# A two-layer graph network on one core: ten score blocks instead of eleven, and x loaded transposed

## The chip, the core and the metric

The kernel runs on one core of one Trainium2 chip. The metric is the device time in microseconds: 1216.45 us, the median of three runs (1216.28 to 1217.08). TensorE is PE here, VectorE DVE, ScalarE ACT, GpSimd POOL, SyncE SP (it only issues DMAs).

## The reference

There are 16 graphs of 512 rows and 384 features (D). Each graph passes a layer norm with relu and then two layers; the result is added to x. Cut to what matters:

```python
h = jnp.maximum(_layernorm(x), 0.0)          # (x - mean) / sqrt(var + 1e-5)
def layer(h, params):
    u = einsum('bid,bjd->bij', h, h) / sqrt(D)          # scores, symmetric
    a = softmax(u);  delta = a * adj
    attn = delta / (sum(delta, -1) + 1e-10)
    hl, hs, hr = h @ wl.T + b_l, h @ ws.T + b_s, h @ wr.T + b_r
    ctx = (attn * upper) @ hl + diag(attn) * hs + (attn * lower) @ hr
    o = (ctx - mean) / sqrt(var + 1e-12) * g + beta
    return relu(o)
x = x + layer(layer(h, p0), p1)
```

## The kernel before

The graphs go in eight pairs, and a pair in four steps: steps 0 and 1 are layer 0 of its two graphs (a and b), steps 2 and 3 layer 1 of the two. The order of every engine's instructions is written out by hand, one Python block for each engine, and semaphores tie them together: an engine works strictly in its own order.

Every fp32 operand is split in a rounded part (_hi) and a rest (_lo), so that a product is three fast matmuls (`products`, L274 to L276). In a step PE does, in this order:

- **Scores** (`scores`, L314): the transposed features ht of one row tile of 128 against a range of columns, in a PSUM bank u_ps for each of the four row tiles. The matrix is symmetric: tile 0 takes all four blocks of 128 columns, tile 1 three, tiles 2 and 3 two each: eleven blocks. ACT copies blocks above the diagonal to u_off.
- **Projections** P(t, n) (`project`): row tile t with weight n. n = 0 and 1 go to proj, n = 2 (self) to hs. There are twelve, in four rotating PSUM banks (rot_ps). A unit must wait until the unit four places ahead of it has been emptied by DVE (`evacuate`).
- **Mirrors** (`mirror`, L332): behind the first two projections, five transposes of u_off fill the missing blocks.
- **M** (`spread_max`, L349), in steps 2 and 3 only, after four projections: the row maxima are turned.
- **T** (`turn_h`, L340): 12 transposes turn the features of the next step's graph. In steps 1 and 2 they turn z, the result of the step before; in steps 0 and 3 they turn x_norm, the layer-normalised x of the graph that comes next in layer 0.
- **Attend** (`attend`), four tiles i: each adds three groups of products of the other tiles' masked scores et with hw, and then those of its diagonal block dg. Its first group waits for all four et_lo, each group for its hw_lo, the diagonal for dg.

Around it, ACT takes exp of the scores, rounds e and proj to et_hi and hw_hi and normalises x (`x_normalise`); DVE masks (L617), forms et_lo (`e_low`, L622), the diagonals (L634), evacuates (L650), ends attend (`finish`) and takes x's statistics (`x_statistics`, L559); POOL forms hw_lo (`proj_low`, L881), the triangles of the diagonal block, dg (`triangles`, L893), and powers for reciprocal deviations (L898, L855).

Of the kernel before, what the change touches and what calls it, by code (L numbers as in the profile page):

```python
# [10 lines left out]
P = 128  # L11


def build_digcn(nc, x, adj_t, w_t, bl, bs, br, ln_w, ln_b, ln_w0_t, ln_b0_t, out):
# [31 lines left out]
    U_FROM = [0, 1, 2, 2]  # L46
    off_at = [0, 3 * P]
# [5 lines left out]
    TWO = (2, 2, 2, 2)  # L53
# [5 lines left out]
    N_HT = (0, 3, 3, 0)  # L59
    N_SHIFT = (1, 1, 0, 0)  # L60
# [4 lines left out]
    with ctx:  # L65
# [22 lines left out]
        u_off = sb("u_off", [P, 5 * P])  # L88
        w_stage = sb("w_stage", [P, 3 * dim])
# [30 lines left out]

        m_rows = u_off[:, 0:n_rows]
        ht_f32 = x_norm[:, :, :].rearrange("p t n -> p (t n)").rearrange("p (k n) -> p k n", n=n_rows)
# [43 lines left out]
        x_norm_loaded = sem("x_norm_loaded")  # L166
        x_loaded = [sem(f"x_loaded_{g}") for g in "ab"]
# [39 lines left out]
        w_stages = [flat(e_sb, 0, 3 * dim), flat(z, 0, 3 * dim), w_stage[:, :]]  # L207
        w_stages += [w_stage[:, :]] * KB
# [5 lines left out]
        def _(sp):  # L214
# [16 lines left out]
            sp.dma_start(x_norm[:, :, :], rows(x, 1)).then_inc(x_norm_loaded, 16)  # L231
# [6 lines left out]
            for g in range(2):  # L238
                sp.dma_start(x_sb[g][:, :, :], rows(x, g)).then_inc(x_loaded[g], 16)
            sp.wait_ge(w_lo0_done, KB)  # L240
            load_w(KB)

            def pair(it, first, last):
                if first:
                    for c in range(1, KB):
                        sp.wait_ge(w_lo1_done, c)
                        load_w(KB + c)
                for g in range(2):
                    s = 2 + g
# [19 lines left out]
        def _(pe):  # L269
# [21 lines left out]
            def step(it, s, first, last):  # L291
# [685 lines left out]
```

## Time and profile before

| what | value |
|---|---|
| time of the profiled execution | 1216.47 us |
| its span | 1214.7 us |
| PE busy | 1200.9 us, 99% |
| DVE busy | 917.0 us, 75% |
| ACT busy | 515.0 us, 42% |
| POOL busy | 561.3 us, 46% |
| PE in the chain that ended last | 93% |

The span is the part of the execution that the profile covers, from the first instruction to the last. Busy time leaves out waits for semaphores, but an instruction that is blocked while it runs counts as busy. Matmuls overlap, so what one costs in a row of them is the distance from start to start and not its duration.

### The profile page before, as it was taken

The numbers are of one execution on the slowest core, as the hardware profiler recorded it, in microseconds if no ns is written. First come the engines' busy times: TensorE is split into PE (matmuls) and PEld (weight loads), VectorE is DVE, ScalarE is ACT, GpSimd is POOL, SyncE is SP. The second block draws the span as 40 slices with busy tenths as digits, with TensorE's granted clock in tenths as the row PEclk, the third lists the DMA queues.
The fourth block names the chain that finished last, engine by engine and source line by source line (L and its number), as shares of the span: only waits on it lengthen the run. The fifth ranks groups of instructions, "written<-read, shape, count | busy, mean of one in ns | idle before, by whom it ended". The sixth has DMA issues, their size and how long they took to land.

```text
span 1214.7 us, 18788 instructions
## 1 busy us (share of the span) xinstructions
PE 1200.9 (99%) x7146; PEld 1178.6 (97%) x7146; DVE 917.0 (75%) x2034; ACT 515.0 (42%) x1061; POOL 561.3 (46%) x624
## 2 busy tenths in 40 slices
PE   9999999999999999999999999999999999999997
PEld 7899999999999999999999999999999999999997
DVE  6567995679955898558985599865997659975688
ACT  4346433355333453334543444434344353434532
POOL 4465353554534545344543354442545424544346
PEclk9999999999999999999999999999999999999999
DMA  8001320012200131001310013100231002210000
GB/s 303 21 21 37 111 79 1 1 61 88 78 2 1 61 113 53 1 1 62 113 53 1 1 62 113 53 1 1 72 103 53 1 1 93 81 53 1 1 27 27
DMA packets 37002, 60.85 MB, mean 50 GB/s; under 512 B 2352, under 2 KB 27952, under 8 KB 36912
## 3 DMA queue, kind: packets, MB, share of 16 engines
q1 hardware_dynamic: 36624, 59.26, 14.8%
q8 instruction: 56, 0.92, 0.3%
q10 hardware_dynamic: 288, 0.39, 0.1%
q14 instruction: 34, 0.28, 0.1%
HBM read 47.06 MB, written 12.58 MB: 49 GB/s over the span
## 4 chain that ended last, share of the span: by engine, by line
PE 93%; DVE 4%; ACT 1%; DMA 1%; issue 1%; POOL 0%; SPq 0%; DVEq 0%
PE rot_ps L275 16%; PE rot_ps L276 16%; PE rot_ps L274 16%; PE u_ps L274 14%; PE u_ps L276 14%; PE u_ps L275 14%; PE rot_ps L340 3%; PE u_ps L332 1%; DMA x_norm<-x_dram 1%; PE rot_ps L349 1%; DVE et_lo L622 0%; DVE proj L650 0%; DVE x_stats L559 0%; DVE z L687 0%; ACT x_norm L419 0%
## 5 line engine op out<-in xcount | busy, mean ns | idle before, releaser
L881 POOL TENSOR_TENSOR hw_lo<-proj,hw_hi 128x384 fp32r<-128x384 f32 x256 | 280.8, 1112 | 323.6 <-ACT hw_hi L471 323.6
L274 PE MATMUL rot_ps<-w_hi,ht_hi 128*128 128x384 f32 x1152 | 389.6, 338 | 1.3 <-DVE proj L650 1.3
L275 PE MATMUL rot_ps<-w_lo,ht_hi 128*128 128x384 f32 x1152 | 385.7, 335 | 0.0
L276 PE MATMUL rot_ps<-w_hi,ht_lo 128*128 128x384 f32 x1152 | 385.5, 335 | 0.0
L274 PEld LDWEIGHTS rot_ps<-w_hi,ht_hi 128*128 128x128 f32 x1152 | 216.5, 188 | 1.6 <-DVE proj L650 1.6
L275 PEld LDWEIGHTS rot_ps<-w_lo,ht_hi 128*128 128x128 f32 x1152 | 216.5, 188 | 0.0
L276 PEld LDWEIGHTS rot_ps<-w_hi,ht_lo 128*128 128x128 f32 x1152 | 216.3, 188 | 0.0
L444 ACT ACTIVATE u_off<-u_ps 128x384 f32<-128x384 f32 x64 | 28.0, 438 | 363.9 <-PE u_ps L276 363.8
L650 DVE TENSOR_TENSOR proj<-rot_ps,bias 128x384 f32<-128x384 f32 x256 | 138.5, 551 | 51.7 <-PE rot_ps L276 51.7
L471 ACT ACTIVATE hw_hi<-proj 128x384 fp32r<-128x384 f32 x256 | 125.5, 518 | 86.5 <-DVE proj L650 85.9
L893 POOL TENSOR_TENSOR dg<-et_hi,tri 128x256 fp32r<-128x256 f32 x128 | 103.4, 808 | 126.7 <-PE u_ps L276 126.7
L706 DVE SCALAR_TENSOR_TENSOR hs<-hs,e_diag,u_ps 128x385 f32<-128x385 f32 x128 | 78.2, 611 | 78.1 <-PE u_ps L276 78.1
L274 PE MATMUL u_ps<-hw_hi,et_hi 128*128 128x386 f32 x384 | 133.1, 347 | 0.5 <-DVE et_lo L622 0.5
L276 PE MATMUL u_ps<-hw_hi,et_lo 128*128 128x386 f32 x384 | 129.8, 338 | 0.0
L275 PE MATMUL u_ps<-hw_lo,et_hi 128*128 128x384 f32 x384 | 129.6, 338 | 0.0
L622 DVE TENSOR_TENSOR et_lo<-e_sb,et_hi 128x512 fp32r<-128x512 f32 x128 | 127.4, 995 | 2.5 <-ACT et_hi L475 2.5
L274 PE MATMUL u_ps<-ht_hi 128*128 128x256 f32 (+2 forms) x384 | 124.6, 325 | 0.7 <-DVE ht_lo L588 0.7
L276 PE MATMUL u_ps<-ht_hi,ht_lo 128*128 128x256 f32 (+2 forms) x384 | 124.6, 324 | 0.0
L275 PE MATMUL u_ps<-ht_lo,ht_hi 128*128 128x256 f32 (+2 forms) x384 | 124.0, 323 | 0.0
L898 POOL TENSOR_TENSOR rstd<-var_eps,minus_half 128x4 f32<-128x4 f32 (+1 forms) x35 | 34.3, 980 | 187.9 <-DVE var_eps L674 187.6
L893 POOL TENSOR_TENSOR dg<-et_lo,tri 128x256 fp32r<-128x256 f32 x128 | 113.7, 888 | 0.0
L650 DVE TENSOR_TENSOR hs<-rot_ps,bias 128x384 f32<-128x384 f32 x128 | 68.9, 550 | 31.9 <-PE rot_ps L276 31.6
(89 smaller groups left out, 2047.6 us busy)
## 6 DMA issues: line engine op xcount, KB each, us to landing
out_dram<-z SPq DMA_DIRECT2D x64, 192.0 KB, 1.9
x_norm<-x_dram SPq DMA_DIRECT2D x15, 768.0 KB, 4.4
adj_a<-adj_t_dram SPq DMA_DIRECT2D x8, 1024.0 KB, 5.3
adj_b<-adj_t_dram SPq DMA_DIRECT2D x8, 1024.0 KB, 5.5
x_a<-x_dram SPq DMA_DIRECT2D x8, 768.0 KB, 4.6
x_b<-x_dram SPq DMA_DIRECT2D x8, 768.0 KB, 4.7
w_stage<-w_t_dram SPq DMA_DIRECT2D x4, 576.0 KB, 5.4
e_sb<-w_t_dram SPq DMA_DIRECT2D x1, 576.0 KB, 4.9
```

Of the source, the lines that this page charges most:

```text
L274: pe.matmul(dst, a_hi, b_hi, start=first and m == 0, stop=False)
L275: pe.matmul(dst[:, 0:b_lo.shape[1]], a_hi, b_lo, start=False, stop=False)
L276: done = pe.matmul(dst, a_lo, b_hi, start=False, stop=last and m == n - 1)
L340: done = pe.transpose(bank(it, s, "T", db)[:, t * P:(t + 1) * P], src[:, t, db * P:(db + 1) * P], ident[:, :])
L444: act.activation(u_off[:, off_at[t]:off_at[t] + width], u_ps[t][:, (t + 1) * P:n_rows], ACT.Copy).then_inc(off_copied, 1)
L471: act.activation(hw_hi[:, t, n, 0:dim], proj[:, t % 2, n, :], ACT.Copy).then_inc(hw_hi_done, 1)
L622: dve.tensor_tensor(et_lo[:, i, :], e_sb[:, i, :], et_hi[:, i, :].bitcast(F32), ALU.subtract).then_inc(et_lo_done, 1)
L650: dve.tensor_tensor(dst, bank(it, s, "P", t, n)[:, 0:dim], bias[:, layer, n, :], ALU.add).then_inc(p_freed, 1)
L706: dve.scalar_tensor_tensor(out=hs[:, i, 0:dim + 1], in0=hs[:, i, 0:dim + 1], scalar=e_diag[:, i:i + 1], in1=u_ps[i][:, 0:dim + 1], op0=ALU ...
L881: pool.tensor_tensor(hw_lo[:, t, n, :], proj[:, t % 2, n, :], hw_hi[:, t, n, 0:dim].bitcast(F32), ALU.subtract).then_inc(hw_lo_done, 1)
L893: pool.tensor_tensor(dg[:, i % 2, part, :, :], block_t.unsqueeze(1).to_broadcast([P, 2, P]), tri[:, :, :], ALU.mult).then_inc(dg_done, 1)
L898: pool.tensor_tensor(rstd[:, cols], var_eps[:, cols], minus_half[:, cols], ALU.pow).then_inc(rstd_done, 1)
```

## The change

Two things change, with what follows from each.

- Scores: row tiles 0 and 1 take three blocks each, 2 and 3 two each, ten in all; tile 3 takes blocks 0 and 3, read and written with a gap. ACT makes four copies to u_off (256, 256, 128, 128 columns) instead of two, and PE six mirror transposes in the order of tiles 1, 2, 3, 0, behind the first projection. The first exp and the first row maximum wait for the mirror of their tile, and DVE evacuates P(0, 0) first.
- x for layer 0: there is no T on x, but for the very first graph. x is loaded a second time, transposed (xt_sb). Its rows' mean and reciprocal deviation come from x in another row layout (four successive rows in a partition), are stored to DRAM and loaded again, spread to all 128 partitions (mean_b and rstd_b, in x_norm). POOL subtracts the mean (`x_centre`, 3 instructions of 128x512), DVE multiplies by the deviation with relu (`x_scale`, 3), ACT rounds (`round_x`), DVE takes the rest (`h_low`). Before, ACT normalised x in place (4) and DVE's h_low read PSUM. The statistics of both next graphs stand in step 1 instead of steps 2 and 3. ht_f32 moves from x_norm to proj, so in steps 1 and 2 `round_h` waits for all eight hw_lo.
- Attend waits for et_lo tile by tile. Three weight chunks of layer 1 are staged in x_b.

```diff
-    UNITS_0 = [("P", *p) for p in PROJ + SELF] + TURN
-    UNITS_1 = [("P", *p) for p in PROJ[:4]] + [("M",)] + [("P", *p) for p in PROJ[4:] + SELF] + TURN
-    ORDERS = [UNITS_0, UNITS_0, UNITS_1, UNITS_1]
+    UNITS_0 = [("P", *p) for p in PROJ + SELF]
+    UNITS_1 = [("P", *p) for p in PROJ[:4]] + [("M",)] + [("P", *p) for p in PROJ[4:] + SELF]
+    ORDERS = [UNITS_0, UNITS_0 + TURN, UNITS_1 + TURN, UNITS_1]
...
-    U_FROM = [0, 1, 2, 2]
-    off_at = [0, 3 * P]
+    SCORED = [slice(0, 3), slice(1, 4), slice(2, 4), slice(0, 4, 3)]
+    OFF_BLOCKS = [slice(1, 3), slice(2, 4), slice(3, 4), slice(0, 1)]
+    OFF_AT = [0, 2, 4, 5]
+    MIRROR_ORDER = (1, 2, 3, 0)
+    MIRRORED = [[(3, 5)], [(0, 0)], [(0, 1), (1, 2)], [(1, 3), (2, 4)]]
...
+        mean_b = x_norm[:, :, :].rearrange("p t n -> p (t n)")[:, 0:n_rows]
+        rstd_b = x_norm[:, :, :].rearrange("p t n -> p (t n)")[:, n_rows:2 * n_rows]
...
-        ht_f32 = x_norm[:, :, :].rearrange("p t n -> p (t n)").rearrange("p (k n) -> p k n", n=n_rows)
+        ht_f32 = proj[:, :, :, :].rearrange("p a b d -> p (a b d)").rearrange("p (k n) -> p k n", n=n_rows)
...
+            def load_stat_rows(graph):
+                sp.dma_start(x_norm[:, :, :], stat_rows(x, graph)).then_inc(x_norm_loaded, 16)
+            def load_xt(graph):
+                sp.dma_start(xt_sb[:, :, :], x_t[graph].rearrange("(k p) n -> p k n", p=P)).then_inc(xt_loaded, 16)
+            def store_x_rows(graph):
+                sp.wait_ge(x_rstd_done, graph + 1)
+                sp.dma_start(rows_dram[graph % 2].rearrange("(q p t) -> p q t", q=2, t=TILES),
+                             x_mv[:, graph % 2, :, :]).then_inc(x_rows_stored[graph % 2], 16)
+            def spread_x_rows(graph):
+                sp.wait_ge(x_rows_stored[graph % 2], 16 * ((graph + 1) // 2))
+                sp.dma_start(flat(x_norm, 0, 2 * n_rows),
+                             rows_dram[graph % 2:graph % 2 + 1, :].to_broadcast([P, 2 * n_rows])).then_inc(x_rows_spread, 16)
...
+                next_a, next_b = it * 2 + 2, it * 2 + 3
+                if not last:
+                    sp.wait_ge(xt_scaled, KB * (next_a - 1))
+                    load_stat_rows(next_a)
+                    sp.wait_ge(ht_lo_done, LEAD_T + at(it, 0, KB, THREE))
+                    load_xt(next_a)
                 if first:
-                    for c in range(1, KB):
-                        sp.wait_ge(w_lo1_done, c)
-                        load_w(KB + c)
+                    sp.wait_ge(w_lo1_done, 1)
+                    load_w(KB + 1)
+                if not last:
+                    sp.wait_ge(x_stats_done, next_a * XS + TILES)
+                    load_stat_rows(next_b)
+                    store_x_rows(next_a)
+                    store_x_rows(next_b)
+                    spread_x_rows(next_a)
...
                         if g == 0:
+                            sp.wait_ge(xt_scaled, KB * next_a)
+                            spread_x_rows(next_b)
+                        else:
                             sp.wait_ge(ht_lo_done, LEAD_T + at(it, s, KB, THREE))
-                        else:
-                            sp.wait_ge(t_ready, LEAD_T + at(it, s, KB, THREE))
-                        sp.dma_start(x_norm[:, :, :], rows(x, it * 2 + (2 + g))).then_inc(x_norm_loaded, 16)
+                            load_xt(next_b)
...
-                    left = U_FROM[t] * P
-                    products(u_ps[t][:, left:n_rows],
+                    which = SCORED[t]
+                    products(blocks(u_ps[t][:, :], which),
                              [(a_t[0][:, kb, lo:hi], a_t[1][:, kb, lo:hi],
-                               a_t[0][:, kb, left:n_rows], a_t[1][:, kb, left:n_rows])
+                               blocks(a_t[0][:, kb, :], which), blocks(a_t[1][:, kb, :], which))
...
-                    if t < TILES - 1:
-                        pe.wait_ge(off_copied, at(it, s, min(t + 1, 2), TWO))
-                    for above in range(U_FROM[t]):
-                        lo = off_at[above] + (t - above - 1) * P
-                        done = pe.transpose(u_ps[t][:, above * P:(above + 1) * P],
-                                            u_off[:, lo:lo + P], ident[:, :])
+                    pe.wait_ge(off_copied, at(it, s, (4, 2, 3, 4)[t], N_OFF))
+                    for column, source in MIRRORED[t]:
+                        done = pe.transpose(u_ps[t][:, column * P:(column + 1) * P],
+                                            u_off[:, source * P:(source + 1) * P], ident[:, :])
...
                 project(0, 0)
+                for t in MIRROR_ORDER:
+                    mirror(t)
                 project(0, 1)
-                for t in range(1, TILES):
-                    mirror(t)
...
+                def round_x(db):
+                    graph = it * 2 + (1 if s == 0 else 2)
+                    act.wait_ge(xt_scaled, KB * (graph - 1) + (db + 1))
+                    act.activation(ht_hi[:, 1 - s % 2, db, :], xt_sb[:, db, :], ACT.Copy).then_inc(ht_hi_done, 1)
...
+                def x_scale(graph, db):
+                    dve.wait_ge(xt_centred, KB * (graph - 1) + (db + 1))
+                    dve.scalar_tensor_tensor(out=xt_sb[:, db, :], in0=xt_sb[:, db, :], scalar=0.0, in1=rstd_b,
+                                             op0=ALU.max, op1=ALU.mult).then_inc(xt_scaled, 1)
...
+                if s == 1 and not last:
+                    x_stats_of(next_a, range(TILES))
+                    x_variance(next_a)
                 if layer == 0:
+                    evacuate(0, 0)
                     mask(0)
-                    evacuate(0, 0)
                     evacuate(0, 1)
                     mask(1)
                     mask(2)
@@ -724,26 +783,30 @@
                     mask(3)
                     e_low(0)
                     evacuate(1, 1)
+                    if s == 1 and not last:
+                        x_stats_of(next_b, range(0, 2))
                     e_low(1)
                     e_low(2)
                     evacuate(2, 0)
-                    if early:
-                        dve.wait_ge(x_norm_loaded, 16)
-                        x_statistics(0)
+                    if s == 1 and not last:
+                        x_stats_of(next_b, range(2, TILES))
                     e_low(3)
+                    if s == 1 and not last:
+                        x_variance(next_b)
...
+            def x_centre(graph):
+                pool.wait_ge(xt_loaded, 16 * graph)
+                pool.wait_ge(x_rows_spread, 16 * graph)
+                for db in range(KB):
+                    pool.tensor_tensor(xt_sb[:, db, :], xt_sb[:, db, :], mean_b, ALU.subtract).then_inc(xt_centred, 1)
...
                 proj_low(1)
+                if s == 0:
+                    x_centre(it * 2 + 1)
+                if s == 2 and not last:
+                    x_centre(it * 2 + 2)
```

POOL in step 0 of the second pair, before. hw_lo<-proj is proj_low, x2 for one row tile, dg is triangles, the memset sets ones.

```order
L881 TENSOR_TENSOR hw_lo<-proj,hw_hi 128x384 x2
L876 MEMSET hs 128x4x2
L881 TENSOR_TENSOR hw_lo<-proj,hw_hi 128x384 x2
L893 TENSOR_TENSOR dg<-et_hi,tri 128x256
L893 TENSOR_TENSOR dg<-et_lo,tri 128x256
L881 TENSOR_TENSOR hw_lo<-proj,hw_hi 128x384 x2
```

The same place in the changed kernel; xt_sb<-xt_sb,x_norm is x_centre.

```order
L937 TENSOR_TENSOR hw_lo<-proj,hw_hi 128x384 x2
L932 MEMSET hs 128x4x2
L937 TENSOR_TENSOR hw_lo<-proj,hw_hi 128x384 x2
L911 TENSOR_TENSOR xt_sb<-xt_sb,x_norm 128x512 x3
L949 TENSOR_TENSOR dg<-et_hi,tri 128x256
L949 TENSOR_TENSOR dg<-et_lo,tri 128x256
L937 TENSOR_TENSOR hw_lo<-proj,hw_hi 128x384 x2
```

Three instructions of 128x512 now stand behind the second tile's hw_lo and ahead of all other hw_lo and of all dg.

DVE in step 1 of the second pair, before, from the first et_lo. proj<-rot_ps is evacuate, diag_junk the diagonal.

```order
L622 TENSOR_TENSOR et_lo<-e_sb,et_hi 128x512
L650 TENSOR_TENSOR proj<-rot_ps,bias 128x384
L622 TENSOR_TENSOR et_lo<-e_sb,et_hi 128x512 x2
L650 TENSOR_TENSOR proj<-rot_ps,bias 128x384
L622 TENSOR_TENSOR et_lo<-e_sb,et_hi 128x512
L634 SCALAR_TENSOR_TENSOR diag_junk,e_diag<-e_sb,ident 128x128
L650 TENSOR_TENSOR proj<-rot_ps,bias 128x384
L634 SCALAR_TENSOR_TENSOR diag_junk,e_diag<-e_sb,ident 128x128 x3
L650 TENSOR_TENSOR proj<-rot_ps,bias 128x384 x2
```

The same place in the changed kernel; x_stats, x_mv and x_var_eps are the statistics of x.

```order
L677 TENSOR_TENSOR et_lo<-e_sb,et_hi 128x512
L705 TENSOR_TENSOR proj<-rot_ps,bias 128x384
L605 BN_STATS x_stats<-x_norm 128x6 x2
L677 TENSOR_TENSOR et_lo<-e_sb,et_hi 128x512 x2
L705 TENSOR_TENSOR proj<-rot_ps,bias 128x384
L605 BN_STATS x_stats<-x_norm 128x6 x2
L677 TENSOR_TENSOR et_lo<-e_sb,et_hi 128x512
L611 BN_AGGR x_mv<-x_stats 128x2 x4
L615 TENSOR_SCALAR x_var_eps<-x_mv 128x4
L689 SCALAR_TENSOR_TENSOR diag_junk,e_diag<-e_sb,ident 128x128
L705 TENSOR_TENSOR proj<-rot_ps,bias 128x384
```

Nine small or middle instructions of the second graph's statistics have come between evacuate(1,1) and evacuate(2,1).

SP at the end of the loads at the start, before.

```order
L239 DMA x_b<-x_dram 128x4x384
L217 DMA w_stage<-w_t_dram 128x1152 x3
L252 DMA adj_a<-adj_t_dram 128x4x512
L257 DMA x_norm<-x_dram 128x4x384
L260 DMA out_dram<-z 128x384 x4
```

And in the changed kernel; rows_dram is the DRAM buffer of means and deviations.

```order
L283 DMA x_a<-x_dram 128x4x384
L245 DMA x_b<-w_t_dram 128x1152
L260 DMA rows_dram<-x_mv 128x2x4
L265 DMA x_norm<-rows_dram 128x1024
L253 DMA x_norm<-x_dram 128x1536
L256 DMA xt_sb<-x_t_dram 128x3x512
```

The store of rows, the load that spreads them, and the statistics' load of the next graph have come behind the last of the first loads; each waits for another engine.

## Rows read from the trace of the kernel before

**Rows 1.** Windows, steps 3, 0, 1: busy us by engine (instructions), clock, DMA
```profile
573.64:611.11 37.47, 37.47 (x226) 36.92 (x226) 35.77 (x84) 15.89 (x34) 17.10 (x19) 1.00 0.29 92
611.11:648.12 37.01, 37.01 (x222) 36.55 (x222) 27.76 (x63) 13.23 (x29) 17.30 (x19) 1.00 0.14 44
648.12:685.13 37.01, 37.01 (x222) 36.55 (x222) 22.25 (x47) 15.66 (x32) 16.42 (x18) 1.00 0.00 1
```

**Rows 2.** Timeline of PE, scores, two projections, mirrors of step 3: start us, duration us
```profile
573.64 0.39 PE L274 MATMUL u_ps<-ht_hi 128*128 128x512 f32 x1
...
575.73 0.34 PE L274 MATMUL u_ps<-ht_hi 128*128 128x384 f32 x1
...
579.46 0.34 PE L274 MATMUL rot_ps<-w_hi,ht_hi 128*128 128x384 f32 x1
...
582.59 0.71 PE L332 MATMUL u_ps<-ident,u_off 128*128 128x128 f32 x5
```

**Rows 3.** Chain in order of time, transposes of x and mirrors: start us, us
```profile
582.75 0.55 PE u_ps L332 x5
...
599.41 1.31 PE rot_ps L340 x12
```

**Rows 4.** Waits of PE: total us, times, longest us
```profile
PEld rot_ps L340 <- ACT x_norm L419: 1.7, 1, 1.7
...
PEld rot_ps L274 <- DVE proj L650: 1.6, 1, 1.6
...
PE u_ps L274 <- DVE et_lo L622: 0.5, 1, 0.5
```

**Rows 5.** Timeline of POOL in step 0
```profile
625.98 1.19 POOL L881 TENSOR_TENSOR hw_lo<-proj,hw_hi 128x384 fp32r<-128x384 f32 x1 [0.23 <-ACT hw_hi L471]
627.14 1.19 POOL L893 TENSOR_TENSOR dg<-et_hi,tri 128x256 fp32r<-128x256 f32 x1
...
632.47 0.74 POOL L893 TENSOR_TENSOR dg<-et_lo,tri 128x256 fp32r<-128x256 f32 x1
633.16 1.99 POOL L881 TENSOR_TENSOR hw_lo<-proj,hw_hi 128x384 fp32r<-128x384 f32 x2
```

**Rows 6.** Timeline of DVE in step 0
```profile
626.46 1.27 DVE L622 TENSOR_TENSOR et_lo<-e_sb,et_hi 128x512 fp32r<-128x512 f32 x1 [0.16 <-ACT et_hi L475]
...
630.79 1.12 DVE L634 SCALAR_TENSOR_TENSOR diag_junk<-e_sb,ident 128x128 f32<-128x128 f32 x1
...
631.84 1.01 DVE L650 TENSOR_TENSOR proj<-rot_ps,bias 128x384 f32<-128x384 f32 x2
```

**Rows 7.** Timeline of PE: end of projections in step 0, attend in step 2
```profile
636.25 1.47 PE L340 MATMUL rot_ps<-ident,x_norm 128*128 128x128 f32 x12
...
711.97 0.42 PE L274 MATMUL u_ps<-hw_hi,et_hi 128*128 128x386 f32 x1
```

**Rows 8.** Timeline of DVE: statistics and means in step 3, evacuate(2,1) in step 1
```profile
574.31 1.01 DVE L559 BATCH_NORM_STATS2 x_stats<-x_norm 128x6 f32<-128x384 f32 x2
...
577.11 0.37 DVE L563 BATCH_NORM_AGGREGATE x_mv<-x_stats 128x2 f32<-128x6 f32 x4
...
666.55 0.55 DVE L650 TENSOR_TENSOR proj<-rot_ps,bias 128x384 f32<-128x384 f32 x1
```

**Rows 9.** Timeline of POOL in step 2
```profile
704.82 5.30 POOL L881 TENSOR_TENSOR hw_lo<-proj,hw_hi 128x384 fp32r<-128x384 f32 x4 [1.35 <-ACT hw_hi L471]
...
710.78 1.18 POOL L893 TENSOR_TENSOR dg<-et_lo,tri 128x256 fp32r<-128x256 f32 x1
```

**Rows 10.** DMA issues, first 45 us, then all: KB each, median us to landing
```profile
x_norm<-x_dram SPq DMA_DIRECT2D x1, 768.0 KB, 6.4
...
out_dram<-z SPq DMA_DIRECT2D x64, 192.0 KB, 1.9
x_norm<-x_dram SPq DMA_DIRECT2D x15, 768.0 KB, 4.4
```

**Rows 11.** Windows: 30 to 35 us of the span
```profile
30.00:35.00 5.00, 3.92 (x23) 3.60 (x21) 4.97 (x14) 0.53 (x1) 2.22 (x2) 1.00 0.00 0
```

More of the change, by code:

```diff
@@ L198, in all_pairs, with blocks, stat_rows @@
                 body(it, it == 0, it == pairs - 1)
+        def blocks(columns, which):
+            return columns.rearrange("p (b c) -> p b c", c=P)[:, which, :]
         def rows(dram, graph):
             return dram[graph].rearrange("(t p) n -> p t n", p=P)
+        def stat_rows(dram, graph):
+            return dram[graph].rearrange("(p t) n -> p t n", t=TILES)
         def flat(tile, lo, hi):
@@ L513, in step @@
                     round_e(3)
-                    if s == 0 and not first:
-                        x_normalise(it * 2 + 2, range(0, 2))
-                else:
-                    row_sum(0)
+                else:
+                    for t in range(TILES):
+                        row_sum(t)
                     round_proj(0)
-                    row_sum(1)
-                    row_sum(2)
-                    row_sum(3)
                     copy_max()
@@ L529, in step @@
                     round_e(1)
-                    if s == STEPS - 1 and not last:
-                        x_normalise(it * 2 + 3, range(0, 2))
                 if first and s == 1:
@@ L537, in step @@
                     round_e(3)
-                if s == 0 and not first:
-                    x_normalise(it * 2 + 2, range(2, TILES))
-                elif s == STEPS - 1 and not last:
-                    x_normalise(it * 2 + 3, range(2, TILES))
                 round_proj(3)
-                if first and s == 0:
-                    x_normalise(2, range(TILES))
                 if not final:
                     for db in range(KB):
-                        round_h(db)
+                        round_h(db) if s in (1, 2) else round_x(db)
                 if first and s == 0:
@@ L601, in step, with x_stats_of @@
                 g, layer = s % 2, s // 2
[L602 to L603 removed]
+                next_a, next_b = it * 2 + 2, it * 2 + 3
+                def x_stats_of(graph, tiles):
+                    if tiles[0] == 0:
+                        dve.wait_ge(x_norm_loaded, 16 * graph)
+                    for t in tiles:
+                        x_statistics(t)
+                def x_scale(graph, db):
+                    dve.wait_ge(xt_centred, KB * (graph - 1) + (db + 1))
+                    dve.scalar_tensor_tensor(out=xt_sb[:, db, :], in0=xt_sb[:, db, :], scalar=0.0, in1=rstd_b,
+                                             op0=ALU.max, op1=ALU.mult).then_inc(xt_scaled, 1)
                 def row_max(t):
[L606 to L609 removed]
+                    dve.wait_ge(u_full, at(it, s, MIRROR_ORDER.index(t) + 1, FOUR))
                     dve.tensor_scalar(e_sb[:, t, :], u_ps[t][:, :], -scale, None, ALU.mult, ALU.min,
@@ L780, in step @@
                         diagonal(t)
-                else:
-                    for t in range(TILES):
-                        evacuate(t, 2)
-                if not final:
+                if s in (1, 2):
                     for db in range(KB):
                         h_low(db)
+                if s == 0:
+                    for db in range(KB):
+                        x_scale(next_a - 1, db)
                 if final:
@@ L807, in step @@
                         centre(i - 1)
-                    if ahead is not None and i in (1, 2):
-                        if i == 1:
-                            dve.wait_ge(x_norm_loaded, (ahead - 1) * 16)
-                        x_statistics(2 * i - 2)
-                        x_statistics(2 * i - 1)
+                    if s in (0, 3) and i < 2:
+                        for db in ((0,), (1, 2))[i]:
+                            h_low(db)
+                    if s == 2 and not last and i in (1, 2):
+                        for db in ((0, 1), (2,))[i - 1]:
+                            x_scale(next_a, db)
                 dve.wait_ge(stats_done, at(it, s, TILES, FOUR))
@@ L902, in step @@
                     pool.wait_ge(den_done, at(it, s, 0, ONE))
+                if first and s == 0:
+                    x_rstd_of(1)
+                if s == 1 and not last:
+                    x_rstd_of(it * 2 + 2)
                 proj_low(0)
@@ L908, in step @@
                     proj_low(2)
-                    if first and s == 0:
-                        x_rstd_of(2)
                     triangles(1)
+                    if s == 1 and not last:
+                        x_rstd_of(it * 2 + 3)
                     proj_low(3)
@@ L946, in step @@
                 rstd_of(slice(0, TILES), 1)
-                if s >= 2 and not last:
-                    x_rstd_of(it * 2 + (s + 1))
             all_pairs(lambda it, first, last: [step(it, s, first, last) for s in range(STEPS)])
```

174 lines of the change are left out of this document (81 added, 93 removed).

## The prediction

> **What bounds the kernel now.** First the page: the span is 1214.7 us, PE is busy in 99% of it, and the chain that ended last is PE for 93%. Then windows of one step each [rows 1]: PE fills all 37.0 or 37.5 us, at a granted clock of 1.00. DVE is busy for 35.8 of 37.5 us in step 3, but for 28 and 22 in steps 0 and 1; POOL for about 17. Then the waits: PE's own are the few of rows 4, 4 us of 1215. So whatever leaves PE is gained, until another engine becomes late, and the question is how much room its feeders have. PE needs two things of them: a free one of the four rotating banks (DVE's evacuations), and for attend et_lo from DVE, hw_lo and dg from POOL. Their dates stand in the timelines, and the main part of this prediction is to compare them with PE's.
>
> **What leaves PE.** Scores: nine 512-wide products of tile 0 take 2.09 us (573.64 to 575.73) [rows 2]; nine 384-wide ones of tile 1, read in the same timeline, 1.59 (575.73 to 577.32), 0.177 each, near the 0.174 of a projection's (3.13 us from 579.46 to 582.59 for eighteen [rows 2]). Tile 0 becomes 384 wide, tile 1 stays: 0.50 us in each of 32 steps, -16.0 us. Tile 3 now reads blocks 0 and 3. No row shows an operand with a gap; between nothing and the price of 384 columns (0.5 a step, +16 us) I take nothing, since 256 columns still stream. Turning x: 12 transposes cost 1.31 us [rows 3], in steps 0 and 3 but not in the last one: 15 x 1.31, -19.65 us. Mirrors: six instead of five, at 0.55/5 [rows 3], 32 x 0.11 = +3.5 us. PE's own work: -32.1 us. The waits of the first pair's step 0, 1.6 and 1.7 us, come from statistics between evacuations and from the normalising of x, and go: -3.3. The 0.5 us for et_lo in the last step goes too, since attend now waits tile by tile [rows 4]. Together -35.9 us.
>
> **What the feeders get.** POOL: three subtractions of 128x512 in steps 0 and 2, behind proj_low(1). DVE: three x_scale in steps 0 and 2, where it waits for attend anyway, and in step 1 all statistics of two graphs; those of steps 2 and 3 go. ACT: two short copies more, no normalising. In steps 2 and 3 the row sums stand together, but copy_max still waits for M, which PE reaches after the same projections, so what follows it keeps its dates.
>
> One POOL subtraction, alone: two hw_lo (384 columns) take 1.99 us, dg (256) 0.69 from start to start (632.47 to 633.16) [rows 5]. With 1.01 for one hw_lo that is 0.98 and 0.69, 0.0022 us a column, 1.25 us for 512 and 3.75 for three.
>
> Beside DVE it is dearer. dg takes 1.19 at 627.14 and 0.74 at 632.47; hw_lo takes 1.19 at 625.98 [rows 5]. On DVE an et_lo takes 1.27 beside them, and a diagonal, with a quarter of its columns, 1.12 [rows 6]. The starts show turns: each of these begins its work when the other engine's instruction ends. They read two tiles of SBUF; two evacuations, which read PSUM, take 1.01 together [rows 6]. The Trainium skill, "SBUF — State Buffer", section "Who interferes with whom", has this as a rule: a DVE instruction with two SBUF inputs and a GpSimd instruction that reads SBUF exclude each other for their whole length. It speaks against this change, since it puts longer instructions of GpSimd among DVE's; by it the time is the forecast's, without it rival 2's. The trace agrees, by rows 5 and 6.
>
> *Step 0* (611.11 to 648.12 [rows 1]). evacuate(0,1) now comes behind the mirrors, 0.66 later; masks and e_low(2) follow about 0.5 later. From there the engines take turns. Before, two dg and one hw_lo (0.7 + 0.7 + 1.0 = 2.4) lie between e_low(2) and diagonal(1), now three subtractions (3.75); then two dg (1.4) stand where POOL had one hw_lo and a gap. 0.5 + 1.35 + about 0.9: evacuate(3,0) starts at 634.6 instead of 631.84 [rows 6] and ends at 635.1. P(2,2), which takes its bank, would start two projections (3.13) before they all end, which is 636.25 [rows 7] + 0.11 for the sixth mirror: 633.2. Stall 2.0 us. POOL's last hw_lo ended at 633.16 + 1.99 = 635.15 [rows 5]; with 3.75 and 1.0 more of turns it is 639.9. Attend now starts at 636.36 + 2.0 and wants it for its third group, six products or 1.05 later, at 639.4: 0.5 more, with the wake-up 0.6. So 2.6 us. Bounds: without turns, 635.15 + 3.5 against 637.4, 1.3; with every subtraction at the contended 1.19 for 384 columns [rows 5], 1.6 for 512, 3.6.
>
> *Step 1* (from 648.12 [rows 1]). The second graph's statistics stand ahead of evacuate(2,1): four in 1.88 (two in 1.01, overlapping) and 0.48 for means and the sum behind them (0.37 for four means) [rows 8], 2.36 in all; 0.25 for exps that start later, 0.3 of turns. evacuate(2,1) goes from 666.55 [rows 8] to 669.45 and ends at 670.0. P(1,2) needs it three projections before their end, which comes 25.14 us after the step's start as in step 0 (636.25 - 611.11): 648.12 + 25.14 - 4.7 + 0.11 = 668.7. Stall 1.35 us; bounds 0.8 (the 2.36 alone) and 2.4. The first graph's statistics fall into DVE's wait for exp and cost nothing.
>
> *Step 2* (from 685.13). POOL idles for 1.35 us behind proj_low(1), until 704.82 [rows 9]; that takes part of the 3.75. Tile 0's last dg ended at 710.78 + 1.18 = 711.96 [rows 9]; 2.4 later is 714.4, and with 0.8 for turns with four et_lo and the diagonals 715.2. PE wants it nine products (1.66) after attend's start at 711.97 [rows 7], and 0.11: 713.7. Stall 1.5 us; bounds 0.6 and 2.5.
>
> *Step 3.* ACT is freed of 2.4 us, but the 1.31 us of PE that hid dg are gone: by the same walk it is 0.25 us late; bounds 0 and 0.5.
>
> Step 0 pays in pairs 2 to 8, steps 1 and 2 in pairs 1 to 7 (the last has no next graph), step 3 in all: seven times 2.6 + 1.35 + 1.5 + 0.25 = 5.7, 39.9 us.
>
> *First pair, step 0.* POOL waits for graph 1's spread rows. x's second load lands 6.4 us after its issue [rows 10], statistics follow, and the small store queues behind loads that run until shortly before 30 us (none from 30 on [rows 11]): landed at 28.8. No row shows a 16-byte store or the spread of one row; by size, 192 KB land in 1.9 us and 768 KB in 4.4 [rows 10], 512 KB in 3.3, so the rows are there at 32.2. Behind them POOL has 3.75, four dg and four hw_lo (6.8) to do: 42.75. Attend's third group comes at 37.6: scores end 6 us after they begin at 11.7, now 0.5 less, attend starts 19.4 later (636.36 less 611.11 + 5.82), the group 1.05 after it. Stall 5.2 us; bounds 3 and 8. In later pairs the rows have over 20 us.
>
> **Sum.** 1216.5 - 35.9 + 5.2 + 39.9 = 1225.7 us. 1216.5 is the profiled execution's own time, and within 0.1 the median. Break-even lies at (35.9 - 5.2)/7 = 4.4 us of stalls a pair.
>
> **Rivals.**
> 1. *Forecast.* The turns add up as walked: 1225.7; its own range is 1214 to 1240. For it: the same walk over steps 0 and 2 of before gives their starts within 0.2 us. Against: it chains some 20 instructions to dates with about 1 us of room.
> 2. *Faster, the work is only inserted.* If DVE and POOL meet less in the new dates, the stalls are 1.3 + 0.8 + 0.6 a pair, 18.9 in all, and 3 in the first: 1216.5 - 35.9 + 21.9 = 1202.5. Its place is e_low(2) to evacuate(3,0) of step 0, its price up to 3 us a pair, and it decides as soon as a pair's stalls are under 4.4. For it: POOL is idle for over half of each step. Against: rows 5 and 6 show the turns already.
> 3. *Faster, all hidden.* The subtractions beat hw_lo's rate and the banks come free in time; 3 us stay in the first pair: 1183.6. Against: 2.2 us more on POOL's chain of step 0 reach PE.
> 4. *Much slower, the way through DRAM.* If store and spread are so slow that POOL waits for them in step 2 too, all that is queued behind x_centre waits: hw_lo, dg, then attend. Over 20 us are left; each microsecond beyond costs 7, so 3 of them give 1247. SP, which waits in order, has adjacency and outputs behind these DMAs, with tens of microseconds.
>
> **Chances.** Forecast 0.52, rival 2 0.28, rival 3 0.12, rival 4 0.08. A difference under 0.2% (2.4 us) can't be told from no change; 0.05 of the forecast's and 0.05 of rival 2's fall there. Faster 0.35, same 0.10, slower 0.55. The range 1194 to 1240 holds the first two.
>
> **What would show it.** After: six mirrors in 0.66 us, tile 0's nine products in 1.59, tile 3's as tile 2's, no transposes of x behind the start. POOL's 512-wide group at 1.3 to 1.7 us each. PE waits for DVE's proj (P(2,2) in step 0, P(1,2) in step 1), for hw_lo in step 0 and dg in step 2. Steps 0 to 3 last 37.9, 38.0, 38.6 and 36.0 us instead of 37.0, 37.0, 37.5 and 37.5. I am wrong if PE is still busy for 99%, or if it waits for a DMA past the first pair.

## The result, and the profile after

The kernel after takes 1219.88 us (median of 7 runs, 1218.83 to 1221.22) against 1216.59 before (7 runs, 1216.28 to 1217.20): ratio 1.0028, 95% interval 1.0016 to 1.0039. It is slower by 3.3 us where 9.2 were forecast. The profiled execution took 1218.83 us, the shortest of the seven; its span is 1217.1.

First the page of the profile: PE is no longer the whole of the span. Engine, busy us, share; then the chain that ended last.

```profile
PE 1178.3 (97%) x6998; PEld 1157.8 (95%) x6998; DVE 982.9 (81%) x2064; ACT 495.1 (41%) x1065; POOL 625.7 (51%) x669
...
PE 49%; DVE 27%; POOL 10%; ACT 7%; issue 5%; DMA 2%; DVEq 0%; POOLq 0%
```

Windows of steps 0 to 3 of pair 5 show where [rows 1 for before]: PE now stands still for 1.1 us in steps 0 and 1 and 0.6 in step 2.

```profile
615.74:652.65 36.91, 35.78 (x212) 35.14 (x212) 31.08 (x59) 11.67 (x27) 20.04 (x21) 1.00 0.27 86
652.65:690.58 37.93, 36.83 (x224) 36.45 (x224) 26.34 (x65) 16.14 (x34) 18.09 (x20) 1.00 0.16 53
690.58:728.58 38.00, 37.37 (x228) 36.84 (x227) 31.09 (x62) 18.95 (x39) 21.29 (x21) 1.00 0.08 29
728.58:764.78 36.20, 36.06 (x216) 35.55 (x215) 34.30 (x73) 13.98 (x32) 16.90 (x18) 1.00 0.28 90
```

The waits of PE answer to [rows 4]: total us, times, longest. They are the three that were forecast, each at its place; two places of hw_lo's nine are the first pair's.

```profile
PE rot_ps L337 <- DVE proj L705: 13.7, 14, 1.3
PE u_ps L337 <- POOL hw_lo L937: 9.1, 9, 4.9
PE u_ps L337 <- POOL dg L949: 4.3, 7, 0.6
```

The timeline of PE has them one by one: P(2,2) and attend's third group in step 0, P(1,2) in step 1, tile 0's dg in step 2 (start us, duration, in brackets the wait ahead).

```profile
638.28 0.44 PE L337 MATMUL rot_ps<-w_hi,ht_hi 128*128 128x384 f32 x1 [0.82 <-DVE proj L705]
643.06 0.41 PE L337 MATMUL u_ps<-hw_hi,et_hi 128*128 128x386 f32 x1 [0.30 <-POOL hw_lo L937]
...
673.90 0.44 PE L337 MATMUL rot_ps<-w_hi,ht_hi 128*128 128x384 f32 x1 [1.10 <-DVE proj L705]
...
719.48 0.45 PE L337 MATMUL u_ps<-hw_hi,dg 128*128 128x386 f32 x1 [0.63 <-POOL dg L949]
```

Where the time went, from the starts of the scores in each trace (us a step, pair 5; the first pair's step 0 apart). The last five columns belong to the experiments below.

| step | before | after | scores_only | centre_late | r_turns | r_all | r_tail |
|---|---|---|---|---|---|---|---|
| 0 | 37.01 | 36.91 | 36.57 | 35.24 | 35.61 | 35.25 | 35.25 |
| 1 | 37.01 | 37.93 | 36.57 | 37.93 | 37.96 | 36.55 | 36.55 |
| 2 | 37.48 | 38.00 | 37.04 | 38.36 | 37.04 | 37.05 | 37.05 |
| 3 | 37.48 | 36.20 | 37.51 | 36.53 | 36.00 | 37.38 | 37.15 |
| first | 40.31 | 44.61 | 39.91 | 36.70 | 45.95 | 36.43 | 36.04 |

In the last pair, which prepares no next graph, steps 1 and 2 take 36.55 and 37.05: these are the lengths without stalls. For step 0, 35.25 is seen in the experiments. For step 3 its parts, each without a stall, add up: scores 5.29, projections up to attend 19.88, and attend 10.58, as in step 0 (10.65 in steps that turn h). That is 35.75, and pair 6 of the kernel after does show 35.74. So a pair loses 1.66, 1.38, 0.95 and 0.45 us, 4.44 in all, and PE's own work is 4.38 less. They cancel. (PE's waits in the views are shorter than these losses: a wait counts from the end of a product of 0.34 us, and in an unbroken row the next one starts after 0.175.)

### The profile page after: what moved, and what is told of

Read it like the earlier page. It is cut to its first block, busy times and chain, and to the rows that moved or that the text cites. A ratio compares the mean times of both kernels' runs of the same rounds, so it can differ in the third digit from the quotient of the medians.

```text
span 1217.1 us, 18750 instructions
## 1 busy us (share of the span) xinstructions
PE 1178.3 (97%) x6998; PEld 1157.8 (95%) x6998; DVE 982.9 (81%) x2064; ACT 495.1 (41%) x1065; POOL 625.7 (51%) x669
## 4 chain that ended last, share of the span: by engine, by line
PE 49%; DVE 27%; POOL 10%; ACT 7%; issue 5%; DMA 2%; DVEq 0%; POOLq 0%
PE u_ps L337 11%; PE u_ps L339 11%; PE u_ps L338 11%; DVE et_lo L677 6%; PE rot_ps L337 5%; PE rot_ps L339 5%; PE rot_ps L338 5%; POOL hw_lo L937 4%; POOL xt_sb L911 3%; DVE proj L705 3%; DVE e_sb L672 3%; DVE u_ps L684 2%; POOL dg L949 2%; DVE hs L705 2%; DVE diag_junk L689 2%
## 5 line engine op out<-in xcount | busy, mean ns | idle before, releaser
L337 PE MATMUL rot_ps<-w_hi,ht_hi 128*128 128x384 f32 x1152 | 390.9, 339 | 13.7 <-DVE proj L705 13.7
L500 ACT ACTIVATE u_off<-u_ps 128x128 f32<-128x128 f32 (+1 forms) x128 | 42.5, 332 | 392.5 <-PE u_ps L339 392.3
L677 DVE TENSOR_TENSOR et_lo<-e_sb,et_hi 128x512 fp32r<-128x512 f32 x128 | 145.0, 1137 | 1.4 <-ACT et_hi L529 1.4
L949 POOL TENSOR_TENSOR dg<-et_hi,tri 128x256 fp32r<-128x256 f32 x128 | 106.4, 831 | 70.2 <-PE u_ps L339 70.2
L954 POOL TENSOR_TENSOR rstd<-var_eps,minus_half 128x4 f32<-128x4 f32 (+1 forms) x35 | 38.7, 1107 | 185.3 <-DVE var_eps L726 185.0
L337 PE MATMUL u_ps<-ht_hi 128*128 128x256 f32 (+1 forms) x384 | 118.8, 309 | 0.7 <-DVE ht_lo L635 0.7
L339 PE MATMUL u_ps<-ht_hi,ht_lo 128*128 128x256 f32 (+1 forms) x384 | 118.8, 309 | 0.0
L338 PE MATMUL u_ps<-ht_lo,ht_hi 128*128 128x256 f32 (+1 forms) x384 | 118.3, 308 | 0.0
L949 POOL TENSOR_TENSOR dg<-et_lo,tri 128x256 fp32r<-128x256 f32 x128 | 108.9, 851 | 0.0
L337 PE MATMUL u_ps<-hw_hi,dg 128*128 128x386 f32 x256 | 88.0, 344 | 4.3 <-POOL dg L949 4.3
```

The lines of the kernel that those rows point to most:

```text
L337: pe.matmul(dst, a_hi, b_hi, start=first and m == 0, stop=False)
L338: pe.matmul(dst[:, 0:b_lo.shape[1]], a_hi, b_lo, start=False, stop=False)
L339: done = pe.matmul(dst, a_lo, b_hi, start=False, stop=last and m == n - 1)
L500: act.activation(u_off[:, OFF_AT[t] * P:OFF_AT[t] * P + width], u_ps[t][:, first_block * P:first_block * P + width], ACT.Copy).then_inc(of ...
L677: dve.tensor_tensor(et_lo[:, i, :], e_sb[:, i, :], et_hi[:, i, :].bitcast(F32), ALU.subtract).then_inc(et_lo_done, 1)
L949: pool.tensor_tensor(dg[:, i % 2, part, :, :], block_t.unsqueeze(1).to_broadcast([P, 2, P]), tri[:, :, :], ALU.mult).then_inc(dg_done, 1)
```

## Experiments

Times are medians, ratios are to the kernel before, run on the same chip; each edit is to the kernel after, but for the first.

**The score blocks alone** (r_scores_only), in the kernel before, with the mirrors' new order and the copies; x is turned as before.

```
-    U_FROM = [0, 1, 2, 2]
+    SCORED = [slice(0, 3), slice(1, 4), slice(2, 4), slice(0, 4, 3)]
```

> The kernel before with ten score blocks alone; x is still turned on TensorE. My theory: the scores lose what the trace after shows, 5.82 - 5.29 = 0.53 us a step, the sixth mirror adds 0.11, nobody waits: 32 x 0.42 = 13.4, so 1216.6 - 13.4 = 1203.2 us. Then the rest of the change (x loaded turned) costs 16 to 17 us. Rival A, the later exps and masks (they wait for the mirrors) make DVE's evacuations late by themselves in step 0: a wait on proj of 0.5 us a pair or more, 1207 or above. Rival B, the feeders had been late for reasons of their own and the loss is in the score blocks: 1216 or more.

1206.20 us, ratio 0.9915 (0.9901 to 0.9930): 10.3 gained, not 13.4. Steps 0 to 2 give 0.44 each, as computed, so neither rival holds: step 0 has no wait for proj behind the first pair, and the scores are not where the time is lost. Step 3 gives nothing back. Its window, PE's waits for dg in the whole run, and DVE at the end of step 2:

```profile
716.49:754.00 37.51, 37.33 (x227) 36.87 (x227) 36.00 (x84) 16.30 (x36) 17.05 (x19) 1.00 0.28 92
...
PE u_ps L280 <- POOL dg L890: 1.0, 6, 0.2
...
714.60 1.02 DVE L560 BATCH_NORM_STATS2 x_stats<-x_norm 128x6 f32<-128x384 f32 x2 [1.29 <-DMA x_norm<-x_dram]
```

PE is held at tile 0's dg in attend: the products with it begin 0.34 us later than in an unbroken row. Followed back in the trace, that dg hangs on POOL's hw_lo, ACT's hw_hi and row sums, and DVE's row, which is busy for 36.0 of the 37.5 us and at the end of step 2 waits 1.29 us for the load of x. So the feeders, not PE, set the end of step 3; which link of that chain would have to give is not shown. By difference the other part of the change costs 13.7 us.

**POOL's subtractions where POOL waits** (r_centre_late).

```
 (behind proj_low(1))
-                if s == 0: x_centre(it * 2 + 1)
-                if s == 2 and not last: x_centre(it * 2 + 2)
 (behind proj_low(3) in step 0, behind triangles(1) in step 2)
+                x_centre(...)
```

> The kernel after, with POOL's three subtractions moved behind the last proj_low in step 0 and behind triangles(1) in step 2, where POOL waits for attend. Theory (turns and insertion ahead of hw_lo and dg make the stalls of steps 0 and 2): both stalls go, 7 x (1.6 + 0.95) = 17.9, and the first pair's waits for hw_lo with the slower clock behind them, 9.2: 1219.9 - 27.1 = 1192.8 us. POOL's subtractions then take 1.25 to 1.3 each in step 0. Rival (the work is too much for the engines wherever it stands): DVE's x_scale then waits for POOL ahead of finish(0), finish and the next step's start slip by 1 us in both steps: 1205 or above, with waits of PE for ht_lo or c_freed at the starts of steps 1 and 3.

1204.73 us, ratio 0.9904 (0.9889 to 0.9919), 12 us above the theory and just under the rival's 1205. Step 0 and the first pair behave as the theory says (35.24, 36.70). Step 2 does not: it is longer by 0.36, and step 3 by 0.33. Timelines of POOL, DVE and PE in step 2:

```profile
706.62 4.35 POOL L911 TENSOR_TENSOR xt_sb<-xt_sb,x_norm 128x512 f32<-128x512 f32 x3
710.94 1.18 POOL L949 TENSOR_TENSOR dg<-et_hi,tri 128x256 fp32r<-128x256 f32 x1
...
708.04 4.63 DVE L713 TENSOR_TENSOR ht_lo<-proj,ht_hi 128x512 fp32r<-128x512 f32 x3
...
713.31 0.44 PE L337 MATMUL u_ps<-hw_hi,dg 128*128 128x386 f32 x1 [1.03 <-POOL dg L949]
```

The subtractions now meet DVE's h_low, both are stretched, and a later tile's dg comes 1.03 us late instead of tile 0's 0.63. Neither theory had this: the rival expected waits for ht_lo or c_freed. The move only changed the partner.

**The second graph's statistics later** (r_stats_late), one behind each evacuation of the self term.

```
-                    if s == 1 and not last: x_stats_of(next_b, range(2, TILES))
                     e_low(3)
 ...
                         evacuate(t, 2)
+                        if s == 1 and not last: x_stats_of(next_b, [t])
```

With them the sum behind the statistics moves, and POOL's power for the deviation goes behind proj_low(3); r_both, r_all, r_all2 and r_tail have this too.

> The kernel after, with the second graph's statistics of step 1 placed one behind each evacuation of the self term instead of ahead of evacuate(2,1). Theory: step 1's wait for proj, 1.38 us, goes in seven pairs: 9.7, 1210.2 us, step 1 at 36.55 us as in the last pair. Rival (DVE is short of time in step 1, wherever the statistics stand): the evacuations that free the banks of the transposes come late instead, 0.5 us or more a pair remain: 1213.7 or above.

1209.73 us, ratio 0.9943 (0.9927 to 0.9960). Step 1 takes 36.56 us; the stall and its price, 10.2 us, are as said.

**The subtractions late in the first pair alone** (r_centre_first).

```
-                if s == 0:
+                if s == 0 and not first:
                     x_centre(it * 2 + 1)
```

> The kernel after, with the three subtractions moved behind the last proj_low in the first pair's step 0 alone, so that hw_lo and dg don't queue behind the rows' way through DRAM. Theory: the waits of 4.9 and 2.0 us and the 1.4 us of slower clock behind them go, and the rest of that stall: 9.2 us, 1210.7. Rival (the rows' way still sets the end of the step, through x_scale ahead of finish(0) and round_x): 3 to 5 us come back as a wait at step 1's start, 1214 or above.

1211.47 us, ratio 0.9959 (0.9944 to 0.9974): 8.4 of the 9.2 us. That step takes 37.47 instead of 44.61, with no wait for hw_lo left in it.

**Both moves** (r_both).

> Both moves together: the subtractions behind the last proj_low (step 0) and behind triangles(1) (step 2), and the second graph's statistics behind the self term's evacuations. If the two stalls are independent, 1204.7 (centre late alone) less 7 x 1.38 = 1195.0 us. Rival (DVE, late by its h_low beside the subtractions in step 2, is what limits, and the stall only moves on): 1199 or above.

1194.81 us, ratio 0.9818 (0.9802 to 0.9835). The two stalls are independent; step 2 keeps its 38.3.

**Spread in step 2** (r_all): one subtraction behind each of triangles(1), (2), (3), beside both moves.

```
                 triangles(2)
+                if s == 2 and not last: x_centre(it * 2 + 2, 1)
                 triangles(3)
+                if s == 2 and not last: x_centre(it * 2 + 2, 2)
```

> As both moves together, but in step 2 one subtraction stands behind each of triangles(1), (2) and (3). Theory from the trace of the first move: three subtractions in a row beside DVE's h_low take 4.35 us and make tile 2's dg 1.0 us late, and make DVE late into step 3 (0.36 us for et_lo); one alone leaves room before each dg. 1195.0 - 7 x (1.3 + 0.35) = 1183.5 us, step 2 at 37.05 to 37.2 us, step 3 at 36.2. Rival (the wait turns up again at x_scale, for which DVE then waits in the middle of its finishes): 1190 or above, with a wait of PE for c_freed or for ht_lo at step 3's start or for et_lo in it.

1191.55 us, ratio 0.9794 (0.9780 to 0.9809), not 1183.5. Step 2 is free of stalls (37.05), and 0.8 of it comes back in step 3: PE waits for the row maxima, which neither side named, and for et_lo, which the rival did.

```profile
719.74 0.65 PE L409 MATMUL rot_ps<-ident,neg_max 128*128 128x128 f32 x4 [0.68 <-DVE e_sb L665]
...
734.40 0.45 PE L337 MATMUL u_ps<-hw_hi,et_hi 128*128 128x386 f32 x1 [0.38 <-DVE et_lo L677]
```

**x_scale one finish later** (r_all2).

```
-                        for db in ((0, 1), (2,))[i - 1]:
+                        for db in ((0,), (1, 2))[i - 1]:
```

> As r_all, with DVE's x_scale of step 2 shifted by one finish: block 0 behind finish(1), blocks 1 and 2 behind finish(2). Theory from the trace of r_all: DVE waits 1.1 us for the second subtraction in the middle of its finishes (two x_scale in 2.37 us instead of 1.29), runs late into step 3, and PE waits there 0.7 us for the row maxima and 0.4 for et_lo. With the wait gone step 3 takes 36.2 to 36.5 us instead of 37.4: 1191.6 - 7 x 1.0 = 1184.6 us. Rival (DVE has no room in step 3 anyway, since the third subtraction still lies beside its finishes): 0.5 us or more of the wait for row maxima stays, 1188 or above.

1191.17 us, ratio 0.9792 (0.9778 to 0.9805): the theory falls. x_scale of one block took 1.78 us instead of 0.68, because it now took its turn against the third subtraction; nothing was won. In step 3 DVE is busy for 35.5 of 37.4 us, and the chain to PE's wait is DVE's row almost without a break.

**DVE's tail moved** (r_tail): in step 2 add_x(2) and add_x(3) go into step 3, ahead of shift_scores(0); otherwise r_all.

> As r_all, with DVE's last two additions of x of step 2 moved into step 3, behind evacuate(1,1), where DVE waits 0.94 us for the copied row maxima. Theory: in step 3 DVE's own row is the limit from the tail of step 2 on; the row maxima come 0.95 us earlier, PE's wait of 0.68 us for them goes, the additions fill a wait, and et_lo comes 0.7 earlier too: step 3 takes 36.7 us instead of 37.4, 1191.5 - 7 x 0.68 = 1186.7 us. Rival (the limit in step 3 is the later chain to et_lo, whatever comes before): the wait moves from the row maxima to et_lo, which then is 1.0 us, and the time stays within 1 us of 1191.5.

1190.20 us (1190.05 to 1191.07), ratio 0.9787 (0.9774 to 0.9801): the best version, 2.1% under the kernel before. It gains 0.23 of the 0.68 us a pair. The wait for the maxima is gone, and the one for et_lo has grown from 0.4 to 1.1 (waits of PE, then DVE's timeline):

```profile
PE u_ps L337 <- DVE et_lo L678: 8.0, 8, 1.1
...
718.70 1.84 DVE L748 SCALAR_TENSOR_TENSOR z<-z,x_a 128x384 f32<-128x384 f32 x2
```

The rival is nearer: DVE's whole row decides step 3, not one date in it. The two additions, 1.02 us before, took 1.84 in their new place.

**The turns by themselves** (r_turns). Two memsets of 512 columns, one behind the other, stand for each subtraction; they write a part of x_norm that nothing reads then, and the mean is not subtracted.

```
-                    pool.tensor_tensor(xt_sb[:, db, :], xt_sb[:, db, :], mean_b, ALU.subtract)
+                    pool.memset(flat(x_norm, 2 * n_rows, 3 * n_rows), 0.0)   (twice)
```

> The kernel after, with each subtraction replaced by two memsets of 512 columns on POOL at the same place, which write and read nothing (the mean is not subtracted): the same insertion of about 1.2 us each, without turns between POOL and DVE. Theory of turns: DVE's et_lo and diagonals beside them take what they take alone (0.6 and 0.3 us), evacuate(3,0) of step 0 ends a microsecond or more earlier, the wait for proj in step 0 goes and the one for dg in step 2 halves: 7 x 1.3 less, 1210.8 us (1208 to 1214). Rival, insertion alone: POOL's time counts and not DVE's; the waits for proj, hw_lo and dg stay within 0.2 us: 1218 or above.

1202.95 us, ratio 0.9886 (0.9872 to 0.9901): 16.9 under the kernel after, where the theory had 9.1 (its range ended at 1208) and the rival 2 at most. In step 0 POOL is held for 3.52 us (624.03 to 627.55), where the subtractions held it for 4.70 (631.38 to 636.08). The first pair's three, beside which DVE only evacuates, took 3.75 (33.41 to 37.16). Beside the memsets DVE's et_lo and diagonals are short; POOL and DVE in this kernel, then in the kernel after:

```profile
624.03 0.52 POOL L912 MEMSET x_norm<- 128x512 f32 x1
...
625.02 0.68 DVE L678 TENSOR_TENSOR et_lo<-e_sb,et_hi 128x512 fp32r<-128x512 f32 x1
625.62 0.28 DVE L690 SCALAR_TENSOR_TENSOR diag_junk<-e_sb,ident 128x128 f32<-128x128 f32 x1
```

```profile
631.38 4.74 POOL L911 TENSOR_TENSOR xt_sb<-xt_sb,x_norm 128x512 f32<-128x512 f32 x3
...
630.70 1.27 DVE L677 TENSOR_TENSOR et_lo<-e_sb,et_hi 128x512 fp32r<-128x512 f32 x1 [0.15 <-ACT et_hi L529]
632.36 1.31 DVE L677 TENSOR_TENSOR et_lo<-e_sb,et_hi 128x512 fp32r<-128x512 f32 x1
633.59 1.37 DVE L689 SCALAR_TENSOR_TENSOR diag_junk<-e_sb,ident 128x128 f32<-128x128 f32 x1
...
637.68 1.01 DVE L705 TENSOR_TENSOR proj<-rot_ps,bias 128x384 f32<-128x384 f32 x2
```

An et_lo takes 0.68 instead of 1.31, a diagonal 0.28 instead of 1.37. Per pair steps 0, 2 and 3 lose 1.30, 0.96 and 0.20 of their length: 2.46 of the 3.06 us by which they are too long in the kernel after. Step 0 keeps 0.36 us and step 3 0.25. At most 0.23 us in each of steps 0 and 2 can be POOL's shorter hold (3.52 against 3.75). The Trainium skill, "SBUF — State Buffer", section "Who interferes with whom", says that a DVE instruction with two inputs in SBUF contends with a GpSimd instruction that reads SBUF, but not with one that only writes it. Both halves are seen here, by the durations above.

**The clock in the first pair** (r_clock_fill). 24 and 10 idle products inside the two waits.

```
+                            if it_first and s == 0 and j > 1:
+                                pe.wait_ge(p_freed, at(it, s, 3 * TILES, N_P))
+                                for _ in range((24, 10)[j - 2]):
+                                    pe.matmul(rot_ps[0][:, 0:dim], ..., start=True, stop=True)
```

> The kernel after, with 24 and 10 idle products on TensorE inside its waits for hw_lo in the first pair's step 0 (a free bank is written, nothing else is changed). Theory: TensorE's granted clock fell after the wait, and that costs by itself: the products behind it take 0.175 us from start to start again instead of 0.32, 1.4 us are saved, 1218.5 us, the two waits' ends staying at 42.0 and 45.2 us. Rival: the slow products come from the feeders (or the clock falls all the same), the time stays at 1219.9.

1218.31 us (10 runs, 1217.90 to 1219.54), ratio 1.0014 (1.0004 to 1.0023): 1.6 us less than the kernel after, but the two intervals overlap (1.0016 to 1.0039 there). The traces say it more surely: the nine products behind the second wait take 1.65 us (45.53 to 47.18) instead of 2.99 (45.25 to 48.24), 1.3 us less. Windows, the granted clock third from the end; the kernel after, then this one:

```profile
42.00:45.20 3.20, 1.27 (x3) 0.76 (x3) 0.00 (x0) 0.00 (x0) 3.10 (x4) 0.50 0.47 196
45.20:50.00 4.80, 4.75 (x19) 4.79 (x20) 1.42 (x3) 0.00 (x0) 1.44 (x2) 0.69 0.00 0
```

```profile
42.00:45.20 3.20, 2.51 (x13) 2.22 (x13) 0.00 (x0) 0.00 (x0) 3.20 (x5) 1.00 0.49 202
45.20:50.00 4.80, 4.47 (x25) 4.50 (x26) 1.88 (x3) 0.00 (x0) 1.61 (x3) 1.00 0.02 3
```

The clock stayed at 1.00 (2.4 GHz) instead of 0.50 (1.2 GHz), and 25 instead of 19 products fit into the last window. The step takes 43.54 us instead of 44.61.

## Why the prediction was off

The places stood: PE's waits came where they were named, for the named releasers. The size did not, 3.3 instead of 9.2 us. The steps that failed are the walk over step 0 (2.6 us, 1.66 came), the turns in step 2 (1.5, 0.95 came) and the first pair's stall (5.2, 9.3 came, with TensorE's clock left out). That the kernel is slower, as forecast, is luck, as shown below. Measured on the profiled execution the forecast is 6.9 us too high, and it splits so (negative where less time passed than forecast):

- *PE's own work*: per pair 4.38 us less, forecast 4.18: -1.4 over seven pairs. Tile 0's nine products take 1.58 us, tile 3's gap costs nothing (its nine take 1.08, tile 2's 1.07). Near. "No row shows an operand with a gap" was settled for zero.
- *Stalls per pair*: 4.44 instead of 5.7, -8.8 us over seven. Step 1 was right (1.38, forecast 1.35), step 3 near (0.45, 0.25), step 2 too dear (0.95, 1.5). The largest miss is step 0, 1.66 instead of 2.6, and in it P(2,2)'s wait for evacuate(3,0): the projections are 1.13 us too long (20.51 for 19.38) where 2.0 was walked, attend 0.53 (11.11 for 10.58) where it was 0.6.
- *First pair*: that step takes 44.61 us. The forecast made it 40.31 - 3.3 - 0.5 - 1.3 + 0.1 + 5.2 = 40.5: +4.1. Where 5.2 us of stall were put, 9.3 came.
- The rest, -0.8, lies in the start and the end and was not followed.

So two terms of the sum were mis-sized, in opposite directions: the stalls of a pair too dear, the first pair too cheap. With the first pair's step at 40.5 us, the profiled execution would have taken 1214.7 us, less than the 1216.47 of before. The forecast of a slower kernel is right only because the second error was there.

*Why step 0 was too dear.* Two errors in one walk. "Masks and e_low(2) follow about 0.5 later" was wrong in sign. The mirrors moved ahead of P(0,1), but the scores ahead of them had become 0.53 us shorter, and I left that out of every date behind them. e_low(2) starts 14.96 us into the step (630.70 - 615.74) instead of 15.35 (626.46 [rows 6] - 611.11): 0.4 earlier, so 0.9 off. P(2,2)'s own date had the same omission and took back 0.5. Then the turns: from e_low(2) to evacuate(3,0) 6.98 us pass, before 5.38 (631.84 - 626.46 [rows 6]). That is 1.60 more, where 1.35 + 0.9 had been walked. The walk had one more round of turns behind the subtractions than came: they end after 4.70 us, 0.95 over their time alone, and of four diagonals only the first took 1.37 us; the others took 0.9 and 0.8. evacuate(3,0) starts at 21.94 into the step, forecast 23.5.

*Why step 2 was too dear.* The "2.4 later" for the inserted subtractions was right: POOL's four hw_lo begin 22.07 us into the step (712.65 - 690.58), before 19.69 (704.82 [rows 9] - 685.13). The further 0.8 for turns did not come: from there to the end of tile 0's last dg POOL takes 6.8 us (to 719.42), before 7.1 (to 711.96 [rows 9]).

*Why the first pair was too cheap.* The rows came nearly when said: the store landed at 29.54 us (forecast 28.8), 8.8 us after its issue, where the median of fifteen is 2.8 [rows 10 have no such store]; the spread took 3.7 us and POOL began at 33.4, forecast 32.2. Behind the subtractions POOL's four dg and four hw_lo took 7.95 us (37.16 to 45.11), forecast 6.8: they had turns with DVE's x_scale. So the last hw_lo was there at 45.1 and not at 42.75, and attend's third group began 7.8 us late and not 5.2 (PE waits 4.9 us ahead of the second group and 2.0 ahead of the third). And no term stood for TensorE's clock: the nine products behind took 2.99 us instead of 1.58, and r_clock_fill gave 1.3 of it back. This step also varies more from trace to trace than anything later. In r_turns the two waits are the same 4.9 and 2.0 us, but the products stay at 0.32 us from start to start until 51.0 us, in the kernel after until 48.2, and the step takes 45.95. In r_stats_late, with the same code in this step, the first wait is 5.8 us and it takes 46.45.

*The rivals.* Rival 2 ("the work is only inserted") erred on the right side: the stalls are smaller than walked. But they are 4.44 us a pair, not its 2.7, and not under the break-even of 4.4, and its reason is wrong. r_turns shows that 2.46 of 3.06 us are turns, and that insertion alone costs 0.36 us in step 0 and nothing in step 2, far under its 1.3 and 0.6. The lower bound of step 0 carried the same missing 0.5 us, about half of that distance. Rivals 3 and 4 did not happen: PE waits for no DMA behind the first pair.

*Not asked in the prediction:* whether PE could use what it was freed of. In step 3 of three kernels it could not: PE waits there for feeders that all hang on DVE's row in r_all and r_tail, and on DVE, ACT and POOL behind the load of x in r_scores_only. But DVE's row is not full by itself. In r_turns step 2 has no stall either, and step 3 takes 36.00 us. In r_all the late subtractions make DVE late: two x_scale take 2.37 us beside them, in the kernel after 1.29. So part of what the moves left in step 3 is turns again, in another place; no run here tells how much.

## What to carry to other kernels

When an edit shortens the first thing in a step, shift every later date of both sides by it before comparing them; the 0.5 us left out here went into every date of step 0, on both sides. Before giving an idle engine work, look at what its neighbour reads in those microseconds, not only at whether it is idle: the same three subtractions cost 1.66 us among et_lo and diagonals (step 0 of the kernel after), nothing among evacuations and x_scale (step 0 of r_centre_late), and 1.3 us among h_low (its step 2). And when a stall is removed, read the next engine's row first: here the moves took 29.7 us off the kernel after and then met DVE. When a forecast comes out on the right side, check the sum term by term all the same: here two errors of opposite sign gave it.

## What was not expected of the hardware

- A wait of 4.9 us on TensorE cost more than its length: the granted clock stood at 0.50 in the next 3.2 us, which hold a second wait of 2.0, and at 0.69 in the 4.8 behind; products took 0.32 us from start to start instead of 0.175. How long they stay slow differs: until 48.2 us in one trace, 51.0 in another with the same two waits.
- Memsets on POOL leave DVE's instructions with two SBUF inputs alone (0.68 and 0.28 us), subtractions make them about two and five times as long (1.31 and 1.37).
- A store of 4 KB took 8.8 us to land in the first 30 us, while loads were under way, and 2.8 us as a rule later. That the loads are the reason is not shown.
- A moving operand of two 128-column blocks with a gap of two between them streams as fast as one without: nine products in 1.08 us, against 1.07.
